# Recommender tower with a two-layer interaction network: twelve small tables gathered jointly for the first five groups

## The reference

```
z = einsum('bhd,bfd->bhfd', hidden, x).reshape(B, h*32, 64)
y = relu(einsum('bcd,oc->bod', z, w) + b)
layer 1: hidden = x;          y[:, :64] is the next hidden, y[:, 64:] is "direct"
layer 2: hidden = y[:, :64];  all 128 are "direct"
```

## Time and profile before

| | |
|---|---|
| median of 3 runs | 1042.82 us (1042.59 to 1043.15) |
| the profiled execution | 1043.1 us, span 1041.3 us |
| busy share of the span | PE 96%, DVE 90%, POOL 90%, ACT 76% |
| mean granted clock of PE | 0.989 |
| DMA | 184 MB, 177 GB/s over the span |

### The profile page before, as it was taken

How to read it: one execution, slowest core, us unless ns; L and a number is a source line. 1 busy time by engine, 2 the same in 40 slices (tenths; PEclk the granted TensorE clock), 3 DMA queues, 4 the chain that set the end, 5 groups by cost and what they waited for, 6 DMA issues and landing times.

```text
span 1041.3 us, 11599 instructions
## 1 busy us (share of the span) xinstructions
PE 1000.6 (96%) x3576; PEld 672.3 (65%) x3576; DVE 938.8 (90%) x806; ACT 795.2 (76%) x956; POOL 934.0 (90%) x315
## 2 busy tenths in 40 slices
PE   2389999999999999999999999999999999999999
PEld 1146666666667666676667676767676767676773
DVE  3079999999999999999999999999999999999981
ACT  5057777778888888888888888888888888788772
POOL 6619999999999999999999999999999999999980
PEclk9599999999999999999999999999999999999999
DMA  6498787778877777777787778777766676767620
GB/s 175 88 236 197 187 198 187 185 185 191 198 186 196 190 191 182 191 188 184 190 201 186 190 184 193 189 183 188 197 168 177 168 186 171 174 175 192 159 71 0
DMA packets 140832, 184.20 MB, mean 177 GB/s; under 512 B 55697, under 2 KB 56337, under 8 KB 140642
## 3 DMA queue, kind: packets, MB, share of 16 engines
q1 hardware_dynamic: 136178, 179.19, 69.9%
q0 software_dynamic: 4096, 4.20, 1.8%
q10 hardware_dynamic: 496, 0.06, 0.0%
HBM read 174.92 MB, written 8.39 MB: 176 GB/s over the span
## 4 chain that ended last, share of the span: by engine, by line
PE 90%; POOL 5%; DMA 1%; issue 1%; SPq 1%; ACT 0%; DVE 0%; ACTq 0%
PE py L809 31%; PE py L832 16%; PE py L818 16%; PE py L819 16%; POOL emb L414 3%; PE py L841 2%; PE py L847 2%; PE py L840 2%; POOL zl L425 2%; PE py L852 1%; DMA xs<-x_dram 1%; SPq L359 0%; PE py L821 0%; PE pzS L911 0%; PE pzB L911 0%
## 5 line engine op out<-in xcount | busy, mean ns | idle before, releaser
L425 POOL TENSOR_TENSOR zl<-zf,zh 128x1536 fp32r<-128x1536 f32 (+1 forms) x183 | 800.7, 4391 | 50.3 <-ACT zh L493 48.7
L695 DVE TENSOR_TENSOR zf<-xs,hid 128x2048 f32<-128x2048 f32 (+1 forms) x256 | 536.3, 2104 | 30.5 <-ACT hid L523 27.0
L493 ACT ACTIVATE zh<-zf 128x2048 fp32r<-128x2048 f32 x189 | 345.9, 1830 | 95.6 <-DVE zf L695 92.6
L809 PE MATMUL py<-zf,wf 128*128 128x512 f32 x820 | 372.6, 592 | 2.7 <-DVE zf L695 2.7
L818 PE MATMUL py<-zh,wh 128*128 128x512 f32 x751 | 292.8, 390 | 0.0
L819 PE MATMUL py<-zh,wl 128*128 128x512 f32 x751 | 292.2, 389 | 0.0
L809 PEld LDWEIGHTS py<-zf,wf 128*128 128x128 f32 x820 | 154.7, 189 | 149.4 <-issue 135.0
L832 PE MATMUL py<-zl,wh 128*128 128x512 f32 x751 | 230.3, 428 | 0.4 <-POOL zl L425 0.4
L832 PEld LDWEIGHTS py<-zl,wh 128*128 128x128 f32 x751 | 140.8, 188 | 60.1 <-issue 32.3
L818 PEld LDWEIGHTS py<-zh,wh 128*128 128x128 f32 x751 | 140.9, 188 | 30.2 <-issue 0.2
L819 PEld LDWEIGHTS py<-zh,wl 128*128 128x128 f32 x751 | 141.0, 188 | 30.0 <-issue 0.2
(11 more groups left out here) (106 smaller groups left out, 665.9 us busy)
## 6 DMA issues: line engine op xcount, KB each, us to landing
xs<-x_dram SPq DMA_DIRECT2D x512, 256.0 KB, 5.0
xs<-x_dram SPq DMA_DIRECT2D x252, 64.0 KB, 2.1
xt_pair<-x_dram SPq DMA_DIRECT2D x128, 64.0 KB
x_pair<-x_dram SPq DMA_DIRECT2D x128, 64.0 KB, 5.1
x_dram<-emb SPq DMA_DIRECT2D x66, 64.0 KB, 5.2
x_dram<-emb SPq DMA_DIRECT2D x22, 96.0 KB, 5.1
emb<-in_tbl,idx POOLq DMA_INDIRECT x128, 5.8
x_dram<-emb SPq DMA_DIRECT2D x4, 384.0 KB, 3.5
```

Of the source, the lines that this page charges most:

```text
L425: pool.tensor_tensor(zl[:, q, first:end], zf[:, s, first:end], zh[:, q, first:end].bitcast(F32), ALU.subtract).then_inc(lo["P"], 1)
L493: act.activation(zh[:, q, first:end], zf[:, s, first:end], ACT.Copy).then_inc(hi, 1)
L695: dve.tensor_tensor(zf[:, slot(u), first:T], left[:, first:T], view(right, at, [[0, T - first], [1, N]]), ALU.mult).then_inc(mult, 1)
L809: mm = pe.matmul(y, wf[:, w, h], zf[:, s, h], start=first and h == first_tile, stop=ends and h == T - 1)
```

## The change

- Tables 20 to 31 (`JOINT` on, `NJ` = 12) are copied behind one another into one DRAM tensor `table_joint` by 12 DMAs of SP. For each of groups 0 to 4 (`JOINT_GROUPS`) the ids of its 8 samples and 12 tables are loaded as 96 rows, DVE adds each table's offset, and POOL gathers all 96 rows with one indirect DMA (`gather_joint`) into `emb_joint`. They are stored to `x_dram` by SP (k = 0, 1: one repeat by SP, one by ACT) as `store_joint`.
- Tables 0 to 19 are gathered first for all of chunk 0 (batches of 12, 5, 3) and only the 40 samples of groups 0 to 4 are stored then. The 12 small tables of the whole chunk ("the rest", batch `REST`) are gathered after the joint gathers: six ahead of the periods, three after low C and three after low B of period 1. From the third on, each waits until the one two before it has landed.
- The samples of groups 5 to 9 and 10 to 15 are stored with all 32 fields by `store_stage(0)`, in SP's iteration 2 with a wait for the rest before and for the store behind it, and by `store_stage(1)` in iteration 3.
- Chunk 1's gathers start in period 2 instead of 0, with four to a period in five periods, then three in four.
- B of group 0 and A of groups 1, 3, 5 become F. `last_whole` is left for A of 7 and 9.
- In SP's order after chunk 0's stores, joint store 2, xe(0) and a wait for that store come ahead of xt_pair(1) and x0_pair(1), and joint stores 3 and 4 with their waits stand ahead of period 0.
- ACT does finish_straight(0) ahead of the copy of x0(1). PE's first warm-up has 3 matmuls instead of 4 (6 passes instead of 8).
- The top weights are loaded in SP's iteration 50; the dense features early, and PE turns them first.

```
-    if name in "PD" or unit in (("A", 0), ("C", 0)):
+    if name in "PD" or g == 0:
         return "F"
+    if name == "A" and g in (1, 3, 5):
+        return "F"
...
-    return name == "A" and g < 11 and g % 2
+    return name == "A" and g in (7, 9)
...
-FIRST_BATCHES = [(0, 0, 12), (0, 12, 12), (0, 24, 5), (0, 29, 3)]
-PER_PERIOD = [[3] * 10 + [2], [2] * 16, [2] * 16]
+JOINT = 20
+NJ = F - JOINT
+JOINT_GROUPS = 5
+FIRST_BATCHES = [(0, 0, 12), (0, 12, 5), (0, 17, 3), (0, JOINT, NJ)]
+REST = len(FIRST_BATCHES) - 1
+STAGES = [JOINT_GROUPS, 10, GC]
+PER_PERIOD = [[4] * 5 + [3] * 4, [2] * 16, [2] * 16]
+FIRST_LATER = 2
...
             sp.dma_start(w1_nat, w1).then_inc(w1_in, 16)
+            sp.dma_start(dense[:], dense_ctx.rearrange("(c p) n -> p c n", p=P)).then_inc(dense_in, 16)
+            for k in range(JOINT_GROUPS):
+                first = ids[NS * k:NS * k + 1, JOINT:JOINT + 1]
+                sp.dma_start(ids_joint[0:NS * NJ, k:k + 1], bass.AP(tensor=first.tensor, offset=first.offset, ap=[[1, NJ], [F, NS], [1, 1]]),
+                             allow_slow_non_contiguous=True).then_inc(ids_joint_in, 16)
...
+            for j in range(NJ):
+                sp.dma_start(table_joint[offsets[j]:offsets[j + 1], :], tables[JOINT + j]).then_inc(tables_joined, 16)
...
+            def store_stage(k):
+                if k == 0:
+                    for n in range(REST):
+                        sp.wait_ge(gathered[n], gathered_count(n))
+                    for i in range(2):
+                        sp.wait_ge(rest_gathered[i], 16 * NJ // 2)
+                lo, hi = NS * STAGES[k], NS * STAGES[k + 1]
+                for i in range(REPEATS):
+                    dst = x_dram[0, i * F:i * F + 1, D * lo:D * lo + 1]
+                    sp.dma_start(bass.AP(tensor=dst.tensor, offset=dst.offset, ap=[[D, hi - lo], [P * D, F], [1, D]]),
+                                 emb[lo:hi, 0, :, :]).then_inc(stage_stored[k], 16)
+
+            def store_joint(k):
+                sp.wait_ge(joint_gathered[k], 16)
+                if k == 0:
+                    sp.dma_start(x32[JOINT:F, :], emb_joint[0:NS * NJ, 0]).then_inc(x32_last, 16)
+                for i in range(1 if k < 2 else REPEATS):
+                    store_joint_rows(sp, k, i)
...
             sp.wait_ge(w_turned, 6)
             sp.wait_ge(x_stored[0], 16 * STORES[0])
+            sp.wait_ge(joint_stored[0], 16 * REPEATS)
             load_xd(0)
+            sp.wait_ge(joint_stored[1], 16 * REPEATS)
             load_x0(1)
             load_xd(1)
+            store_joint(2)
+            load_xe(0)
+            sp.wait_ge(joint_stored[2], 16 * REPEATS)
             load_xt_pair(1)
             load_x0_pair(1)
-            load_xe(0)
             load_x0(2)
+            for k in range(3, JOINT_GROUPS):
+                store_joint(k)
+            for k in range(3, JOINT_GROUPS):
+                sp.wait_ge(joint_stored[k], 16 * REPEATS)
             for g in range(G):
+                if g == 2:
+                    store_stage(0)
+                    sp.wait_ge(stage_stored[0], 16 * REPEATS)
+                if g == 6:
+                    sp.wait_ge(stage_stored[1], 16 * REPEATS)
+                if g == 50:
+                    load_top()
...
+                landed = gathered[n % BATCH_SEMS]
+                if n == REST:
+                    landed = rest_gathered[i % 2]
+                    if i > 1:
+                        pool.wait_ge(landed, 16 * (i // 2))
...
+            def gather_joint(k):
+                if k == 0:
+                    pool.wait_ge(idx_joint_ready, 1)
+                    pool.wait_ge(tables_joined, 16 * NJ)
+                pool.indirect_dma_start(
+                    out=emb_joint[0:NS * NJ, k, :], out_offset=None, in_=table_joint[:],
+                    in_offset=bass.IndirectOffsetOnAxis(ap=idx_joint[0:NS * NJ, k:k + 1], axis=0),
+                ).then_inc(joint_gathered[k], 16)
...
-                for i in range(m):
+                if n == REST:
+                    for k in range(JOINT_GROUPS):
+                        gather_joint(k)
+                for i in range(m - 6 if n == REST else m):
                     gather(n, i)
...
+            finish_straight(0)
             copy_x0(1)
-            finish_straight(0)
...
-            warm_up(4, py1[:])
+            warm_up(3, py1[:])
```

More of the change, by code:

```diff
@@ L393, in _ @@
                     store_batch(batch_of(g - 1))
+                if g == 3:
+                    store_stage(1)
                 if g + 1 < G:
@@ L410, in gather @@
                     pool.wait_ge(x_stored[c - 2], 16 * STORES[c - 2])
-                if i == 0 and n >= BATCH_SEMS:
+                    if c == 2:
+                        for stored in stage_stored:
+                            pool.wait_ge(stored, 16 * REPEATS)
+                landed = gathered[n % BATCH_SEMS]
[3 more added lines that the diff above has]
+                        pool.wait_ge(landed, 16 * (i // 2))
+                if i == 0 and n >= BATCH_SEMS and n - BATCH_SEMS != REST:
                     pool.wait_ge(gathered[n % BATCH_SEMS], gathered_count(n - BATCH_SEMS))
@@ L437, in _ @@
                     gather(n, 1)
+                if g == 1:
+                    for i in range(NJ - 6, NJ - 3):
+                        gather(REST, i)
                 low(("B", g))
+                if g == 1:
+                    for i in range(NJ - 3, NJ):
+                        gather(REST, i)
                 if n is not None:
                     gather(n, 2)
+                    gather(n, 3)
         @block.scalar
@@ L638, in _ @@
             dve.memset(wS[:].bitcast(F32), 0.0).then_inc(cleared, 1)
+            for j in range(NJ):
+                dve.memset(first_row[:, NS * j:NS * j + NS], float(offsets[j])).then_inc(rows_set, 1)
+            dve.wait_ge(eye_in, 16)
+            dve.wait_ge(rows_set, NJ)
+            dve.tensor_tensor(first_row[0:NS * NJ], first_row[0:NS * NJ], ident[0:NS * NJ, 0:NS * NJ], ALU.mult).then_inc(rows_set, 1)
+            dve.wait_ge(rows_set, NJ + 1)
+            dve.tensor_reduce(first_rows[0:NS * NJ], first_row[0:NS * NJ], AX_X, ALU.add).then_inc(rows_set, 1)
+            dve.wait_ge(rows_set, NJ + 2)
+            dve.tensor_copy(first_rows_int[0:NS * NJ], first_rows[0:NS * NJ]).then_inc(rows_set, 1)
+            dve.wait_ge(rows_set, NJ + 3)
+            dve.wait_ge(ids_joint_in, 16 * JOINT_GROUPS)
+            dve.tensor_tensor(idx_joint[0:NS * NJ], ids_joint[0:NS * NJ], first_rows_int[0:NS * NJ].to_broadcast([NS * NJ, JOINT_GROUPS]),
+                              ALU.add).then_inc(idx_joint_ready, 1)
+            dve.wait_ge(dense_turned, 1)
+            dve.wait_ge(cleared, 7)
+            dve.tensor_copy(zd[0:16], px0[0:16]).then_inc(s_low, 1)
             done = 0
@@ L772, in _ @@
             pe.wait_ge(eye_in, 16)
+            pe.wait_ge(dense_in, 16)
+            for c in range(NC):
+                tr = pe.transpose(px0[0:16, P * c:P * c + P], dense[:, c, :], ident[:])
+            tr.then_inc(dense_turned, 1)
             pe.wait_ge(w0_doubled, 8)
@@ L781, in _ @@
             pe.transpose(pzS[:, 0:P], sym16, ident[:]).then_inc(w_turned, 1)
-            pe.wait_ge(top_in, 16 * 8)
-            for c in range(NC):
-                tr = pe.transpose(px0[0:16, P * c:P * c + P], dense[:, c, :], ident[:])
-            tr.then_inc(dense_turned, 1)
             def bank(u):
@@ L889, in _ @@
                 main(("C", g))
-                for name in "DB" if g == 0 else "BD":
-                    main((name, g))
+                main(("B", g))
+                main(("D", g))
                 late(("C", g))
```

98 lines of the change are left out of this document (62 added, 36 removed).

## The result

| | before | after |
|---|---|---|
| median | 1042.72 us (1042.27 to 1043.15, 6 runs) | 1066.48 us (1061.84 to 1073.60, 6 runs) |
| ratio | | 1.0237 [1.0213, 1.0261] |
| profiled execution | 1043.1, span 1041.3 | 1070.1, span 1068.3 |

1040.0 was forecast. The profiled execution is 27.0 us longer; 26.4 of it are lost ahead of 235 us, and from 296 us on PE is late by a constant 27.0.

What follows compares the result with a forecast made beforehand. PE is fully busy from 240 to 710 us, so late A2, waiting for POOL, moves the end. -5.5 + 1.0 + 1.7 = -2.8 from 1043.1 gives 1040.3; the median, 0.3 lower, 1040.0 us; range 1035 to 1046.5.

Steps and rivals of the forecast that it cites:

- Step 1: Group 0's start: x0 needs fewer gathers, so spreads start at 35.8 and PE's A0 at 49.1 instead of 62.93, -13.8 us.
- The late copy: Rival, chance 0.06: the table copy lands at about 40, x0 moves only 3 us; +4 to +7, about 1048 us.
- Step 2: SP's loads ahead of tail(1): DVE's pair product is 3.9 us late, tail(1) at 58.7, PE's gain there -10.8.
- "by bytes" bound: In SP's loads for the pair product: by bytes alone (3.98 MB) the last would land at 55.7, against 55.1.
- Step 3: POOL in period 1: low parts and two groups of three gathers let late A2 start at 95.4 instead of 100.92, -5.5.
- L: Landing time of the first gather in each group of three in period 1, taken as 3.0 and 2.4 us.
- the slower rival: Chance 0.14: two-at-a-time gathers land as slowly as gathers in the loop; at 5.5 us landing time +5.8, 1048.6 us.
- Step 4: store_stage(0) waits for the last gathers and holds up xd(4), so PE waits for P4: +1.7.
- Step 5: PE's own work: B0, A1, A3, A5 in whole fp32; A3 and A5 add 0.5 each, +1.0.
- "nothing": Terms put at no cost: the later top loads in period 50 (0 to 1 us) and four gathers to a period.

Runs made afterwards that it cites:

- x2: The changed kernel without the 12 table copies, joint gathers reading table 20 for all twelve tables: 1053.56 and 1054.78 us, also 1069.97 and 5918.9.
- x15: x12 with x11's gathers, dense transposes first, ACT's x32 loads behind its third weight copy, SP taking four of the first eight: 1044.85 us.
- x1: The changed kernel with PE's dense transposes and DVE's copy of them behind the weights, as before: 1052.83 us.
- x5: The kernel before, unchanged, profiled once more: 1042.28 us in one run.
- x8: x1 with all twelve rest gathers ahead of the periods, none in period 1: 1052.60 us.
- x10: The kernel before with one gather of chunk 0 in flight at a time: 1089.18 us in one run.
- x17: x15 with joint store 2 moved up on SP's queue, from behind xd(1) to behind xd(0): 1045.40 us.
- x11: x8 with chunk 1's gathers from period 1 on, three to a period, four in periods 3 and 5 only: 1050.91 us.
- x13: x8 with the changes of x11 and x12 together and the second stage store moved as in x9: 1048.79 us.
- x14: x13 with SP instead of ACT issuing the first eight loads of x32: 1046.19 us.
- x9: x1 with the second stage store at the end of period 4, behind xe(5), instead of in period 3 ahead of xe(4): 1056.74 us.
- x3: The kernel before with the 12 table copies added, unused: 1042.7 us.
- x4: The changed kernel with the table copies in packets of 2 KB: 1058.22 us.
- x12: x8 with POOL starting the rest gathers only behind group 0's spreads: 1049.27 us.

## Why the prediction was wrong

**Step 1 failed**: "x0 earlier, PE's A0 at 49.1". The rows behind it were right (gathers, copies, joint gather 0 at 29.42; the spreads at 36.10 in x2; A0 at 51.94 in x15). What it took for granted is that PE's signals reach ACT and DVE at once, because they did in the one profiled execution of before. While POOL issues gathers 1.25 us apart, and 2 to 6 us beyond the last, they come up to 22 us late (after, x1, x2, x5, x8; not in x10, and not in that one profile of before, which was luck). The kernel before has the same lateness in x5 at no cost; its idle start was the cover. The change brought its path into that stretch: the copies of the weights with ACT's loads behind them, SP's loads, the spreads. Cost: 18.6 us at A0, of the 29.8 between the forecast of the profiled execution (2.8 below before) and its 27.0 above.

**The late copy** did not come: no wait at joint gather 0. The Trainium skill's rule on the largest divisor ("DMA: Bandwidth & Descriptors", the section on why a DMA increments its semaphore by 16) gave an estimated 212 GB/s for the copies; the window of 18 to 20 us moved 405, and each copy went out as 16 packets of 20,000 or 16,000 bytes, so the page's own exception, a contiguous copy split anew, is what the trace agrees with.

**Step 2** (pair product late): tail(1) was forecast to come out 3.0 us worse than A0. After, behind a late A0, it is 2.8; in x15, the nearest to that A0, it is 5.0, as PE waits 4.44, and the clock costs some 2.6 more (5.49 us busy at 0.52 of it), which the step left out. Its "by bytes" bound, 19.7 us from xd(0)'s issue, was the term that counts: the pair product starts 19.8 us behind that issue in x15, and 21.0 in x17, with the store earlier.

**Step 3** (POOL in period 1): L was taken as 3.0 and 2.4, and the first gathers landed after 5.9 and 2.3, so the chain from low C1 to late A2 took 24.8 us instead of 21.5; in x1, where the third gather starts 3.4 and 2.7 us behind the first (6.1 and 2.7 after), 22.0. The term was mis-sized by 3 us; the mechanism was right, and the slower rival's landing time (5.5) came in the first group alone.

**Step 4** (stage wait): +1.7 forecast. PE waits 2.55 at P4 after, and the six matmuls behind take 4.51 us instead of 2.73, as the granted clock is 0.66 over 134 to 139 us, so +4.3; x8, in which nothing waits for the stage, has neither.

**Step 5 and "nothing"**: four gathers to a period were put at nothing. PE waits 1.79 us for low A4 after, 1.70 in x8; with three it waits 0.37 in x11, but 1.89 in x13. Between tail(5) and tail(6) 3.95 us are lost after, of which A5 in whole fp32 is 0.5. The rest is shared by POOL and by xe(4) behind the second stage store (DVE waits 2.88 us there after); moving either alone or both did not remove it, so how it divides stays open. The top loads in period 50 cost nothing: the offset is 27.01 on both sides of it.

## What to carry to other kernels

Before work is moved into a stretch in which an engine was idle, ask whether signals cross that stretch in time, and take more than one profiled execution to see it: here an idle start hid late signals. Rank the moved waits by what stands behind them in program order: x14, which takes eight loads out from behind ACT's copies, has a median 2.6 us below x13's (whose runs spread over 9.4 us), while moving transfers alone (x9, x17) gained nothing. A wait of PE can cost twice, once as itself and once for the lower clock behind it, as at P4 after and at tail(1) in x15; behind late A4's 1.79 us the clock stayed at 1.00.

## What the runs showed of the hardware

- PE's signals and SP's issues are slow together in the stretch in which POOL gathers one table after the other. In x2 SP's instructions start at 36.37, 37.77, 39.17, 40.57, 41.97 and 42.67, steps of 0.70 us or twice that, and DVE hears of PE's spreads at such steps.
- The trace keeps few records of semaphore updates in that stretch, and they come at the same step. Counted over 24 to 44 us:

```
before 512   after 28   x1 28   x2 29   x3 34   x4 29   x5 29   x10 (one gather at a time) 156
```

28 or 29 in 20 us is one in 0.70 us. Of the kernels that gather every 1.25 us, the profile of before is the only one that kept its records, and the only one with all signals in time. The Trainium skill ("NOTIFIC — the notification-queue block", the section on overflow and its three behaviours) says that the block that writes such records holds its producers up rather than lose one inside. That would fit the common step; but records are missing here, not only late, and every timed execution has a recorded span and clock, so no run shows whether one without records has late signals. What in the chip carries the lateness stays open. That it ends with the gathers is shown (x12 against x8, x15 against x1); that gathers one at a time are free of it rests on one run of x10, beside one profile of before that was free of it with gathers 1.25 us apart.
- 12 copies from DRAM to DRAM with 3.65 MB take 13 us beside the weights' loads, and cost the kernel before nothing (x3).
